# Two attention layers and two feed-forward layers on one core: a written-out order for the first unit of the last stage

## The reference

```
x = x + tanh(g_xattn[0]) * attention0(layernorm(x), ctx)      # per row, over 16 x 16 heads and dims
x = x + tanh(g_ffn[0])   * experts(layernorm(x))              # one shared and one chosen of 8 GEGLU experts
x = x + tanh(g_xattn[1]) * attention1(layernorm(x) as queries, ctx as keys and values)
x = x + tanh(g_ffn[1])   * butterfly_ffn(layernorm(x))        # 256 -> 1024, gelu, -> 256
```

## Time and profile before

| | |
|---|---|
| median of 3 runs | 770.26 us (768.25 to 772.27) |
| profiled execution, its own time | 768.17 us |
| its span | 766.4 us |
| TensorE busy | 697.5 us (91%) |
| VectorE busy | 607.5 us (79%) |
| ScalarE busy | 380.2 us (50%) |
| POOL busy | 416.6 us (54%) |
| mean granted clock of TensorE | 0.98 |

### The profile page before, as it was taken

The page is one execution under the profiler, slowest core; times in us unless marked ns, Lnnn a source line. Parts: engine busy times, 40 slices in busy tenths (PEclk is TensorE's granted clock), DMA queues, the critical chain, the costliest instruction groups (busy, mean ns, idle before and its releaser), DMA issues.

```text
span 766.4 us, 12694 instructions
## 1 busy us (share of the span) xinstructions
PE 697.5 (91%) x4347; PEld 585.7 (76%) x4347; DVE 607.5 (79%) x910; ACT 380.2 (50%) x682; POOL 416.6 (54%) x304
## 2 busy tenths in 40 slices
PE   6659999999999899889999999999976999999996
PEld 4438888878887788567777777777865999989996
DVE  4789999999999945799978887887787767677653
ACT  2323433433433321366666777666643575555643
POOL 3898888888889880406987666665032101110000
PEclk9959999999999999999999999999998999999999
DMA  9501010011036012232354416000010101000000
GB/s 285 202 28 29 28 29 27 27 34 48 28 97 289 8 62 69 69 138 97 123 193 189 189 29 248 28 22 21 15 36 27 35 21 56 29 28 8 15 15 21
DMA packets 28642, 56.43 MB, mean 74 GB/s; under 512 B 3408, under 2 KB 24656, under 8 KB 27440
## 3 DMA queue, kind: packets, MB, share of 16 engines
q1 hardware_dynamic: 23408, 47.64, 17.4%
q0 software_dynamic: 1872, 5.11, 2.5%
q10 hardware_dynamic: 3312, 3.02, 1.2%
HBM read 48.55 MB, written 7.21 MB: 73 GB/s over the span
## 4 chain that ended last, share of the span: by engine, by line
PE 50%; DVE 19%; POOL 12%; issue 10%; ACT 7%; DMA 1%; DVEq 1%; POOLq 0%; ACTq 0%
PE bank L733 20%; PE bank L742 16%; POOL PRODV L619 8%; PE bank L988 8%; PE bank L750 4%; DVE PRODQ L1540 2%; POOL PRODV L621 2%; DVE SLOT_r L1917 2%; DVE bank L1549 2%; DVE PRODV_r L1917 2%; DVE bank L1630 2%; DVE STC L2005 1%; ACT L1446 1%; ACT XS L1446 1%; ACT L1277 1%
## 5 line engine op out<-in xcount | busy, mean ns | idle before, releaser
L619 POOL TENSOR_TENSOR PRODV<-SHARED 128x2048 f32<-128x2048 f32 x32 | 144.7, 4522 | 28.8 <-DVE bank L1630 25.0
L733 PE MATMUL bank<-ROWS,SLOT 128*128 128x128 f32 x1024 | 122.8, 279 | 0.0
L733 PEld LDWEIGHTS bank<-ROWS,SLOT 128*128 128x128 f32 x1024 | 120.4, 195 | 0.8
L712 POOL TENSOR_TENSOR RS<-VE,MHALF 128x2 f32<-128x2 f32 x16 | 13.1, 819 | 151.1 <-DVE VE L2012 151.1
L733 PE MATMUL bank<-SLOT,XST 128*128 (+1 forms) x184 | 82.9, 593 | 0.5 <-ACT XST L1344 0.5
L621 POOL TENSOR_TENSOR PRODV<-PRODV 128x1024 f32<-128x1024 f32 x32 | 74.7, 2335 | 2.5
L1549 DVE TENSOR_REDUCE bank<-PRODQ 128x256 f32<-128x4096 f32 x16 | 70.7, 4419 | 0.1
L1540 DVE TENSOR_TENSOR PRODQ<-bank,SHARED 128x4096 f32<-128x4096 f32 x16 | 70.6, 4413 | 0.0
L636 POOL DMA_INDIRECT XS<-normal_rows,INV x23 | 27.4, 1192 | 71.2 <-PE bank L750 49.9
L1917 DVE TENSOR_TENSOR PRODQ_r<-SLOT,ROWS_r 128x1024 fp32r<-128x1024 f32 x44 | 63.6, 1446 | 0.0
L733 PE MATMUL bank<-SLOT,HA 128*128 128x256 f32 x256 | 58.3, 381 | 2.4 <-DVE HA L1738 2.4
(11 more groups left out here) (269 smaller groups left out, 1828.1 us busy)
## 6 DMA issues: line engine op xcount, KB each, us to landing
SLOT<-wexp SPq DMA_DIRECT2D x9, 3072.0 KB, 11.5
ROWS<-xT SPq DMA_DIRECT2D x16, 128.0 KB, 2.2
SHARED<-ctxT SPq DMA_DIRECT2D x16, 128.0 KB, 2.4
X<-x SPq DMA_DIRECT2D x16, 128.0 KB, 2.4
normal_rows<-ROWS SPq DMA_DIRECT2D x16, 128.0 KB, 1.7
WET<-ctxT SPq DMA_DIRECT2D x4, 512.0 KB, 8.4
out<-X SPq DMA_DIRECT2D x16, 128.0 KB, 1.7
expert_rows<-YS ACTq DMA_DIRECT2D x12, 128.0 KB, 1.7
```

The lines of the kernel that those rows point to most:

```text
L619: gp.tensor_tensor(o, pr, v, ALU.mult).then_inc(s["av_prod"], 1)
L733: last = pe.matmul(dst, lhs(k), rhs(k), start=(k == 0), stop=(k == chunks - 1))
```

## The change

The first unit gets functions of its own, `first_unit`, on TensorE, ScalarE and VectorE, and `unit` is called for u = 1 to 7 alone, without the flag has_up. In the first unit the order is now:

- TensorE: the turns of unit 1's rows come behind scores(1), ahead of attend(0), and queries(1) comes ahead of attend(1).
- ScalarE: the copy of unit 1's turned rows comes ahead of the exponentials of tile 1.
- VectorE: lower_rows(1) comes ahead of largest(1), lower_queries(1) ahead of attended(1). next_rows(2) and next_stats(2) come behind attended(1) and norm_eps(0), the first ahead of norm_rows(0, 2) and the second behind it.
- POOL: the root for unit 0's second norm comes ahead of the root for unit 2's first, and gather(3) behind both.

In units 1 to 7 the order on TensorE, ScalarE and VectorE is the one of before, and so is the order of the ring.

```diff
+            uses.append(("queries", 1))
-            for u in range(UNITS + 1):
+            for u in range(1, UNITS + 1):
...
         def sweep_cd(unit):
-            for u in range(UNITS):
-                unit(u, u > 0, u > 1, u + 1 < UNITS, u + 2 < UNITS,
+            for u in range(1, UNITS):
+                unit(u, u > 1, u + 1 < UNITS, u + 2 < UNITS,
                      u > 1 and u % 2 == 1 and u + 1 < UNITS)
...
             roots(1, 0, "c_eps", "c_rstd")
-            for u in range(UNITS):
+            gather(2)
+            roots(0, 2, "d_eps", "d_rstd")
+            roots(2, 0, "c_eps", "c_rstd")
+            for u in range(1, UNITS):
...
+            def first_unit():
+
+                scores(0)
+                fold(3)
+                flip_weights(0)
+                scores(1)
+                flips(PB[0], 0, 1, "c_xn", "c_xT")
+                attend(0)
+                flip_weights(1)
+                queries(1)
+                attend(1)
...
+            def first_unit():
+
+                weights(0)
+                fold(3)
+                flipped_weights(0)
+                copies(PB[0], 1, "c_xT", XN3T, "c_xT_hi")
+                weights(1)
+                flipped_weights(1)
+                queries(1)
...
+            def first_unit():
+
+                largest(0)
+                lower_fold(3)
+                norm_rows(1, 0, "c_rstd", "c_xT", "c_xn")
+                shares(0)
+                lower_rows(PB[0], 1, "c_xT_hi", XN3T, XN3TL, "c_xT_sb")
+                largest(1)
+                attended(0)
+                shares(1)
+                lower_queries(1)
+                attended(1)
+                norm_eps(0, 2, "d_agg", "d_eps")
+                next_rows(2)
+                norm_rows(0, 2, "d_rstd", "d_xT", "d_xn")
+                next_stats(2)
+                norm_rows(2, 0, "c_rstd", "c_xT", "c_xn")
```

More of the change, by code:

```diff
@@ L389, in ring_order @@
                     ("queries", 0), ("fold", 2), ("fold", 3)]
-            for u in range(UNITS + 1):
+            uses.append(("queries", 1))
+            for u in range(1, UNITS + 1):
                 if u >= 2:
                     uses.append(("down", u - 2, 1))
-                if u:
-                    uses += [("up", u - 1, i) for i in range(4)]
+                uses += [("up", u - 1, i) for i in range(4)]
                 if u > 1 and u % 2 and u + 1 < UNITS:
@@ L398, in ring_order @@
                     uses.append(("queries", u + 1))
-                if u and u < UNITS:
+                if u < UNITS:
                     uses.append(("down", u - 1, 0))
@@ L1116, in attend, with unit @@
                       lambda k: (V1[n // TB % 2][:, k, :], V1L[n // TB % 2][:, k, :]), TB, c["av_done"])
-            def unit(u, has_up, has_down, has_next, has_second, has_values):
+            def unit(u, has_down, has_next, has_second, has_values):
                 scores(2 * u)
-                if u == 0:
-                    fold(3)
                 if has_down:
                     down(u - 2, 1)
-                if has_up:
-                    flips(PB[5], 2, u - 1, "d_xn", "d_xT")
+                flips(PB[5], 2, u - 1, "d_xn", "d_xT")
                 flip_weights(2 * u)
                 scores(2 * u + 1)
-                if has_up:
-                    up(u - 1, 0)
+                up(u - 1, 0)
                 attend(2 * u)
-                if has_up:
-                    up(u - 1, 1)
+                up(u - 1, 1)
                 flip_weights(2 * u + 1)
@@ L1136, in unit @@
                     flips(PB[0], 0, u + 1, "c_xn", "c_xT")
-                if has_up:
-                    up(u - 1, 2)
-                    up(u - 1, 3)
+                up(u - 1, 2)
+                up(u - 1, 3)
                 attend(2 * u + 1)
@@ L1145, in unit @@
                     queries(u + 1)
-                if has_up:
-                    down(u - 1, 0)
+                down(u - 1, 0)
+            def first_unit():
[8 more added lines that the diff above has]
+                attend(1)
             def last_rows():
@@ L1201, in _ @@
             fold(2)
+            first_unit()
             sweep_cd(unit)
@@ L1473, in flipped_weights, with unit @@
                     .then_inc(c["pT_hi"], 1)
-            def unit(u, has_up, has_down, has_next, has_second, has_values):
+            def unit(u, has_down, has_next, has_second, has_values):
                 weights(2 * u)
[L1478 to L1481, removed]
+                copies(PB[5], u - 1, "d_xT", XN4T, "d_xT_hi")
                 flipped_weights(2 * u)
                 weights(2 * u + 1)
-                if has_up:
-                    hidden(u - 1, 0)
-                    hidden(u - 1, 1)
+                hidden(u - 1, 0)
+                hidden(u - 1, 1)
                 flipped_weights(2 * u + 1)
@@ L1489, in unit @@
                     copies(PB[0], u + 1, "c_xT", XN3T, "c_xT_hi")
-                if has_up:
-                    hidden(u - 1, 2)
-                    hidden(u - 1, 3)
+                hidden(u - 1, 2)
+                hidden(u - 1, 3)
                 if has_values:
@@ L1497, in unit @@
                     queries(u + 1)
-                if has_second and u and u % 2 == 0:
+                if has_second and u % 2 == 0:
                     context(u // 2 + 1)
+            def first_unit():
[6 more added lines that the diff above has]
+                queries(1)
             for n in range(4, KF):
@@ L2079, in attended, with unit @@
                 norm_stats(m, 2 + m % 2, m, "d_stats", "d_agg")
-            def unit(u, has_up, has_down, has_next, has_second, has_values):
+            def unit(u, has_down, has_next, has_second, has_values):
                 largest(2 * u)
-                if u == 0:
-                    lower_fold(3)
-                    norm_rows(1, 0, "c_rstd", "c_xT", "c_xn")
                 if has_down:
                     finish_ring(u - 2, 1)
-                if has_up:
-                    lower_rows(PB[5], u - 1, "d_xT_hi", XN4T, XN4TL, "d_xT_sb")
+                lower_rows(PB[5], u - 1, "d_xT_hi", XN4T, XN4TL, "d_xT_sb")
                 shares(2 * u)
                 largest(2 * u + 1)
-                if has_up:
-                    lower_hidden(u - 1, 0)
+                lower_hidden(u - 1, 0)
                 attended(2 * u)
-                if has_up:
-                    lower_hidden(u - 1, 1)
+                lower_hidden(u - 1, 1)
                 shares(2 * u + 1)
@@ L2103, in unit @@
                     next_stats(u + 2)
[L2104 to L2106 removed]
+                lower_hidden(u - 1, 2)
+                lower_hidden(u - 1, 3)
                 attended(2 * u + 1)
@@ L2116, in unit @@
                     norm_rows(u + 2, 0, "c_rstd", "c_xT", "c_xn")
-                if has_second and u and u % 2 == 0:
+                if has_second and u % 2 == 0:
                     lower_context(u // 2 + 1)
-                if has_up:
-                    finish_ring(u - 1, 0)
+                finish_ring(u - 1, 0)
+            def first_unit():
[14 more added lines that the diff above has]
+                norm_rows(2, 0, "c_rstd", "c_xT", "c_xn")
             dve.wait_ge(bcd_ready, 2)
```

## The result

The changed kernel takes 774.84 us (median of 5 runs, 773.11 to 776.33) against 770.26 us; the ratio is 1.005 with a 95% interval of 1.0033 to 1.0067. It is slower by about half a percent. Forecast were 771.9 us and a loss of 1.64: the median lies 0.14 us above the top of the stated range (770.26 times the ratio, 774.1, lies inside), and the loss is 4.6 us between the medians and 3.9 by the ratio, not 1.6.

What follows compares the result with a forecast made beforehand. A chain through all engines to flip_weights(2), behind largest(2) on VectorE, was taken to bound the edited stretch. Largest(2) moves from 590.36 to 592.00, +1.64 us, clock difference 0: 770.26 + 1.64 = 771.9 us, range 769.0 to 774.7.

Steps and rivals of the forecast that it cites:

- Where the gain went: First unit: scores(2) starts 2.58 us earlier, but VectorE's queue ahead of largest(2) makes that 1.64 us later.
- The first root: POOL's root for norm_rows(0, 2), ahead of largest(2): taken as 0.72 us, of which 0.98 with its start lies bare.
- The other bound: POOL's root takes 1.08 us after long idleness, adding 0.36 us, or 0.72 if both roots are long.
- fits into that wait and costs nothing: VectorE's next_rows(2), 0.74 us, runs during the wait for POOL's first root at no cost; otherwise 0.74.
- The clock step: TensorE at flip_weights(2) and scores(3): half clock at the restart in both kernels, a difference of 0.
- shifts as a whole: Everything behind flip_weights(2), some 173 us from 593.74 on, is unchanged and moves together; otherwise the prediction fails.
- Rival 1: VectorE reaches largest(2) as soon as scores(2) are complete, so the 2.58 us gain carries through: 767.7 us; chance 0.05.
- Rival 2: TensorE's clock stays full until 593.74; flip_weights(2) and scores(3) save 1.64 us: 770.3 us, no change; chance 0.13.
- Rival 3: Clock falls early, slowing flip_weights(1), queries(1) and attend(1): +2.8, in all +4.4 us, 774.7 us; chance 0.10.
- Rival 4: Longer roots (0.36 to 0.72 us) or longer half clock (0.65): up to +1.4 on top, 772.3 to 773.3; chance 0.12.
- The rule on throttled time: Skill's price for half clock: a stretch growing from 6.6 to 8.4 us costs 0.9 us more, an upper bound.

Runs made afterwards that it cites:

- Largest(2) first: Changed kernel with largest(2) directly behind norm_eps(0), and next_rows(2), next_stats(2), norm_rows(2) behind largest(3): 768.80 us, ratio 0.998 to the kernel before.
- third profile: Kernel before, unedited, timed against itself once more in the last set: 771.46 us, ratio 1.0017, tail from scores(0) to the end 191.46 us.
- all six orders: The changed kernel and five edited orders, ratios to the kernel before: changed 1.005 to 1.0078, the others 1.0022, 1.0017, 1.0007, 0.998 and 0.9963.
- the second set of the changed kernel: Changed kernel, unedited, timed again against the kernel before: 775.79 against 770.79 us, ratio 1.0078, tail 195.08 us.
- statistics early: Changed kernel with next_rows(2) and next_stats(2) back ahead of lower_queries(1), POOL's roots in their old order: 772.51 us, ratio 1.0022 to the kernel before.
- statistics behind: Changed kernel with largest(2) behind norm_rows(0, 2), then next_stats(2) and norm_rows(2): 771.90 us, ratio 1.0017 to the kernel before.
- roots exchanged: Kernel before with only POOL's root for unit 0's second norm ahead of unit 2's, gather(3) behind both: 771.31 us, ratio 1.0007.
- the order with the rows first alone: Kernel before with only unit 1's rows turned, copied and lowered early; queries, statistics and roots in old places: one profile, tail 194.45 us.
- both orders that gained: Largest(2) first, 768.80 us, ratio 0.998; and the same with largest(1) also ahead of lower_rows(1), 767.84 us, ratio 0.9963.

## Why the prediction was right or wrong

**Where the gain went: right, and nearly to the hundredth.** scores(2) was forecast 12.8 us after scores(0), and it was 12.80; flip_weights(1) 1.36 us later, and it is 8.93 against 7.55 (1.38). The change removes the 2.13 us wait. The work queued ahead of largest(2) gives more back. Largest(2) first, with the same TensorE order, turned the loss into a gain, which shows it.

**The first root was mis-sized.** The prediction's term is 0.72 us from the row with 10.43 us of idleness, with 1.08 as the other bound, put down to idleness. It measured 1.15. The cause is next_rows(2) beside it: 1.15 us in each of the four profiles with that neighbour (three of the changed kernel, one with the statistics behind), 0.72 in the three orders that have it elsewhere, at 11.4 to 12.3 us of idleness. So the step that next_rows(2) "fits into that wait and costs nothing" is wrong; it costs 0.43 us. The other bound, 1.08, was near by luck: that root too was long for its neighbour, and not for its idleness. Largest(2) is 2.15 us later than in the profile before (19.43 against 17.28), where 1.64 was forecast; the root accounts for nearly all of the rest (1.64 + 0.43 = 2.07).

**The clock step does not hold in every execution, and it can be the larger part of what the forecast lacks.** The prediction took "half clock at the restart in both kernels, so a difference of 0". This holds for the two profiles compared first: tail +1.76, since the fallen clock came back 0.3 us sooner in the changed kernel. There the part from flip_weights(2) on shifts as a whole within 0.4 us (174.30 and 173.92), as the prediction asked. But the kernel before also runs at full clock through the same place, as its third profile shows, with scores(0) within 0.02 us of where the changed kernel had it, and there that part is 172.64 us. Between these two the difference in the tail is 195.38 - 191.46 = 3.92 us. The changed kernel has 6.7 us with only four turns in them (593.88 to 600.58), and its clock was at half at the restart in all three profiles. The fall costs it 1.2 to 1.4 us in L3 (3.33 to 3.50 from flip_weights(2) to largest(3), against 2.09 at full clock), and 1.6 in the other one (3.71). The sum in this light: 19.43 - 17.07 = 2.36 us for largest(2), and some 1.3 for the clock, together 3.7.

That the tail of 191.5 is the usual one of the kernel before is an inference, from the table's last two columns. Against 191.5 the tails agree with the whole times of all six orders, or nearly (the second set of the changed kernel lies 0.5 us outside). Against 193.2 they would be +1.9, +0.1, -0.4, -1.6, -4.0 and -5.0, and all six lie outside their intervals. The comparison has an offset of its own, though: the kernel before against itself came out 1.2 and 1.3 us longer, and with that much taken off, 193.2 fits most of the intervals too. Against the timed copy of the kernel before in the same set, the medians differ by +4.3 and +3.4 (changed), +1.1 (statistics early), +0.4 (statistics behind), -0.2 (roots exchanged) and -2.7 us (largest(2) first). All six lie nearer to the tails less 191.5, within 0.9 us, than to the tails less 193.2, and a tail of 191.8 fits them best, an estimate from twelve runs or fewer each. So the kernel before seems to keep its clock more often than not, though two of its three profiles had fallen. How often it falls stays open, and with it how much of the loss, beyond the 2.2 to 2.4 us by which largest(2) is later, is the clock.

**The rivals.** Rival 1 (the earlier scores carry through) did not happen, and largest(2) first shows that it was one reordering away. Rival 2 (full clock at the restart) was looked for on the wrong side: the changed kernel did not keep its clock in any profile, the kernel before did in one of three. Rival 3 (half clock early) did not occur in the changed kernel, but did in the order with the rows first alone. Rival 4's price for the root came true by another cause. That the loss by the ratio, 3.9 us, lies inside the range is partly luck: the range reaches that far for rival 3, which did not happen in this kernel. The rule on throttled time, cited there as an upper bound, puts 0.9 us on a longer stretch at half clock in the changed kernel; what the profiles show is a stretch that is missing in one execution of the kernel before.

**The change itself** puts two things ahead of largest(2) that no engine waits for before largest(3): next_rows(2) and next_stats(2) with their root. VectorE idles 3.72 us behind largest(3) (608.58 in its timeline), and that is where both orders that gained put them.

## What to carry to other kernels

When an order is changed to feed one engine sooner, follow the next engine's queue to the instruction that the following stage waits for: the matmuls came 2.6 us earlier, and the maximum over them 2.2 us later. Put statistics for a later unit into a wait that the trace shows, and not ahead of the next maximum. A clock level read in one profile of the kernel before is not a constant: take two or three profiles before counting it as equal on both sides. Where an instruction is long, look at what the other engines run beside it before putting it down to idleness.

## What the runs showed of the hardware

A root of two columns on POOL takes 1.15 us while VectorE runs `scalar_tensor_tensor` with two inputs of 512 numbers per partition from SBUF beside it, and 0.72 while it runs nothing, or a maximum that reads a bank. Beside a `tensor_tensor` with two such inputs it takes 1.08 us (606.68 in the kernel before). The Trainium skill states this (SBUF — State Buffer, section "Who interferes with whom"): a VectorE instruction with two SBUF inputs contends with a GpSimd instruction that reads SBUF. The trace agrees, with 0.43 us. Applied to next_rows(2), the rule would have raised the forecast; the row at 606.68 (1.08 us against 0.69 to 0.72) would have given the price, 0.4 us.

The granted clock falls or does not fall at the same place in the same code. Behind a wait of 2.13 us it was at half within 1.6 us of the restart in two profiles; behind one of 2.14 us it stayed full in a third. The price of the fall was 1.6 us between flip_weights(2) and largest(3).
